# An attention and feed-forward block on one core: heads in 64-row tiles, preparation batch by batch through memory, four slots of rows

## What is computed

```
mod = silu(c) @ wmod                      # per batch: sa, ca, ga, sb, cb, gb; |ga|, |gb| at least 0.25
h   = layernorm(x) * (1 + ca) + sa
q, k, v = split(h @ W_qkv + b_qkv)        # 16 heads of 8 channels each
att = softmax(q @ k.T) / sqrt(128)        # per head, 256 x 256
x   = x + ga * (concat(att @ v) @ W_out + b_out)
h   = layernorm(x) * (1 + cb) + sb
hq  = h rounded to a 6-bit grid in blocks of 32 with a scale of their own; the weight likewise
out = x + gb * (hq @ Wq.T + bias)
```

## Time and profile before

| what | us |
|---|---|
| median of 3 runs | 349.7 |
| lowest and highest run | 349.1, 350.29 |
| profiled execution: span from first to last instruction | 349.2 |
| TensorE busy | 304.0 |
| VectorE busy | 239.4 |
| ScalarE busy | 218.5 |
| GpSimd busy | 173.1 |

### The profile page before, as it was taken

The page is one execution under the profiler, slowest core; times in us unless marked ns, Lnnn a source line. Parts: engine busy times, 40 slices in busy tenths (PEclk is TensorE's granted clock), DMA queues, the critical chain, the costliest instruction groups (busy, mean ns, idle before and its releaser), DMA issues.

```text
span 349.2 us, 8125 instructions
## 1 busy us (share of the span) xinstructions
PE 304.0 (87%) x2506; PEld 216.6 (62%) x2506; DVE 239.4 (69%) x580; ACT 218.5 (63%) x404; POOL 173.1 (50%) x336
## 2 busy tenths in 40 slices
PE   3635698999899997999799997999899989999952
PEld 1204585767576765677576856677676758686521
DVE  4584587578856894779557992779677955886334
ACT  8683055876567765776477654776677645667720
POOL 4360133266736662566636672567556442546540
PEclk9955569999989998999899996999999987999995
DMA  4155365436552555345542555245544554001000
GB/s 132 32 110 115 112 178 111 113 110 174 107 132 93 159 107 122 104 154 101 112 100 94 168 116 120 90 151 103 113 126 139 107 109 126 32 19 34 18 17 15
DMA packets 23700, 36.46 MB, mean 104 GB/s; under 512 B 3422, under 2 KB 10734, under 8 KB 23670
## 3 DMA queue, kind: packets, MB, share of 16 engines
q1 hardware_dynamic: 23302, 35.43, 40.4%
q0 software_dynamic: 368, 0.66, 1.1%
HBM read 9.25 MB, written 2.13 MB: 33 GB/s over the span
## 4 chain that ended last, share of the span: by engine, by line
PE 40%; SPq 29%; DMA 16%; POOL 4%; issue 4%; DVE 3%; ACT 2%; DVEq 0%; ACTq 0%; POOLq 0%
SPq L326 24%; PE ps_o L903 10%; PE ps_p L888 9%; PE ps_p L874 8%; DMA qk_parts<-qk_parts 7%; DMA q_pad<-maxT 7%; PE ps_pre L930 3%; POOL qk_parts L371 2%; SPq L412 2%; PE ps_post L960 2%; SPq L401 2%; PE ps_o L946 1%; PE ps_post L974 1%; PE ps_post L968 1%; DMA q_pad<-qk_parts 1%
## 5 line engine op out<-in xcount | busy, mean ns | idle before, releaser
L762 DVE TENSOR_REDUCE neg_max<-ps_p 128x2 f32<-128x512 f32 x256 | 167.3, 685 | 72.7 <-PE ps_p L874 72.3
L629 ACT ACTIVATE probs<-ps_p 128x512 f32<-128x512 f32 x256 | 145.6, 595 | 82.1 <-PE ps_p L888 79.9
L874 PE MATMUL ps_p<-k_rep,q_pad 96*128 96x256 f32 x512 | 128.2, 338 | 12.1 <-DMA q_pad<-qk_parts 11.7
L888 PE MATMUL ps_p<-q_pad,k_rep 98*128 98x256 f32 x512 | 108.4, 296 | 12.5 <-DMA q_pad<-maxT 12.5
L874 PEld LDWEIGHTS ps_p<-k_rep,q_pad 96*128 96x128 f32 x512 | 84.6, 205 | 46.4 <-issue 35.0
L888 PEld LDWEIGHTS ps_p<-q_pad,k_rep 98*128 98x128 f32 x512 | 82.5, 198 | 16.8 <-issue 14.1
L903 PE MATMUL ps_o<-probs,v_aug 128*32 128x256 f32 x1024 | 82.3, 407 | 0.2 <-ACT probs L629 0.2
L903 PEld LDWEIGHTS ps_o<-probs,v_aug 128*32 128x32 f32 x1024 | 22.6, 112 | 20.2 <-issue 3.1
L530 POOL TENSOR_TENSOR wout_b<-wout_sc,modb 128x128 f32<-128x128 f32 x16 | 7.3, 459 | 49.7 <-DMA modb<-mod_rows_dram 49.6
L494 POOL CAST max_parts<-neg_max 128x16 fp32r<-128x16 f32 x32 | 6.3, 198 | 39.9 <-DVE neg_max L762 39.2
L356 POOL TENSOR_TENSOR hq<-h,rs 128x256 fp8e4<-128x256 f32 x15 | 9.3, 617 | 25.0 <-DVE rs L808 12.8
(11 more groups left out here) (107 smaller groups left out, 356.1 us busy)
## 6 DMA issues: line engine op xcount, KB each, us to landing
q_pad<-qk_parts SPq DMA_DIRECT2D x123, 64.0 KB
qk_parts<-qk_parts SPq DMA_DIRECT2D x14, 512.0 KB, 3.5
k_rep<-qk_parts SPq DMA_DIRECT2D x31, 192.0 KB
modb<-mod_rows_dram SPq DMA_DIRECT2D x16, 256.0 KB, 3.7
x_early<-in_L_attn_x_dram SPq DMA_DIRECT2D x8, 256.0 KB, 3.4
x_late<-in_L_attn_x_dram SPq DMA_DIRECT2D x8, 256.0 KB, 3.4
out_dram<-out_sb SPq DMA_DIRECT2D x16, 128.0 KB, 1.9
k_rep<-qk_parts SPq DMA_DIRECT2D x15, 128.0 KB
```

What stands on the lines that cost most here:

```text
L629: act.activation(probs[:, v % 2, u % 4, :], ps_p2[:, u % 2, :], ACT.Exp).then_inc(exp_done, 1)
L762: dve.tensor_reduce(neg_max[:, half, :, h % HALF], ps_p1[:, P1_BANK[h], :].rearrange("p (q k) -> p q k", q=QT), AX_X, ALU.max, negate=True ...
L874: ins = pe.matmul(ps_p1[:, P1_BANK[h], t * T:(t + 1) * T], q_pad[0:ROWS, par, h, e, t * P:(t + 1) * P], k_rep[0:ROWS, par, g, e, :], start ...
L888: ins = pe.matmul(ps_p2[:, u % 2, t * T:(t + 1) * T], k_rep[0:ROWS + 2, par, g, e, t * P:(t + 1) * P], q_pad[0:ROWS + 2, par, h, e, :], st ...
```

## The change

- **Row tiles.** Each head has 64 rows of its own: 32 rows of q and k parts (four combinations of parts, 8 channels), rows that stay at zero in q and at one in k, and two rows of maxima, 62 and 63. Even heads lie on partitions 0 to 63, odd heads on 64 to 127. `scores1` uses 62 rows, `scores2` 64. `q_rows` and `k_rows` replace `q_pad` and `k_rep` and have four slots, one per batch.
- **Order.** `scores1` runs 20 heads ahead (`LEAD`) where it ran 16 ahead. Both kinds go through the heads in the order 0, 2, 4, 6, 1, 3, 5, 7 and so on (`HEAD`), the matmuls of both kinds alternate one by one, and all other TensorE work stands behind every second head. `values` now comes in 16 instructions throughout.
- **Preparation.** Statistics, normalisation, q, k and their parts run per batch, in tiles of 256 tokens, three batches ahead of the step. x is loaded once and stays (`x_all`). Batches 0 and 1 are prepared ahead of the loop, batch 0 alone first, with x scaled by VectorE.
- **Layout.** SyncE stores each batch's parts in memory off chip (`parts_dram`) and reads them back from there with two DMAs for q and four for k, which also double them. The maxima of half a batch are placed by two DMAs.
- The modulation rows have four buffers (two before), and the loop is written out in full, without registers.

```diff
-GROUPS = [(0, 3), (3, 3), (6, 2), (8, 3), (11, 3), (14, 2)]
-ROWS = 96
-P1_BANK = [0, 1, 2, 0, 1, 0] + [2, 0, 1] * 3 + [2]
+QUAD = 4 * D
+ROWS1 = 62
+ROWS2 = 64
+LEAD = 20
+RING = 4
+P1_BANKS = 3
+P2_BANKS = 2
+FIRST = 2
+HEAD = [8 * (u // 8) + 2 * (u % 4) + (u % 8) // 4 for u in range(16)]
...
+    parts_dram = nc.dram_tensor("parts_dram", [NB, 2, 2, D, 2, HALF, T], F32, kind="Internal").ap()
...
-        qk_parts = sb("qk_parts", [P, 2, 2, 4, TP], F32R)
-        q_pad = sb("q_pad", [P, 2, H, 2, T], F32R)
-        k_rep = sb("k_rep", [P, 2, len(GROUPS), 2, T], F32R)
+        x_all = sb("x_all", [P, NB, QT, E])
+        qk_parts = sb("qk_parts", [P, 2, 2, 2, T], F32R)
+        q_rows = sb("q_rows", [P, RING, HALF, T], F32R)
+        k_rows = sb("k_rows", [P, RING, HALF, T], F32R)
...
+        def at1(b, s):
+            return divmod(16 * b + s + LEAD, 16)
...
+            def store_part(c, kind):
+                if c < FIRST:
+                    sp.wait_ge(first_low, 2 * c + kind + 1)
+                else:
+                    sp.wait_ge(low_ready, 2 * (c - FIRST) + kind + 1)
+                sp.dma_start(parts_dram[c, kind].rearrange("r d u i t -> i (r d) u t"),
+                             qk_parts[:, c % 2, kind, :, :].bitcast(F32)).then_inc(parts_stored[kind], 16)
+            def lay_out(c, kind):
+                wait(sp, (parts_stored[kind], 16 * (c + 1)), (p2_full, 16 * (c - RING + 1)))
+                if c < RING:
+                    sp.wait_ge(rows_filled[c], 2)
+                for r in range(2):
+                    part = parts_dram[c, kind, r].rearrange("d u i t -> d u (i t)")
+                    if kind == 0:
+                        dst = q_rows[64 * r:64 * r + QUAD, c % RING, :, :].rearrange("a i t -> a (i t)")
+                        sp.dma_start(dst.bitcast(F32), part.unsqueeze(2).to_broadcast([D, 2, 2, HALF * T])
+                                     ).then_inc(laid_out[c % RING], 16)
+                    else:
+                        for u in range(2):
+                            dst = k_rows[64 * r + u:64 * r + QUAD:2, c % RING, :, :].rearrange("a i t -> a (i t)")
+                            sp.dma_start(dst.bitcast(F32), part[:, u:u + 1, :].to_broadcast([D, 2, HALF * T])
+                                         ).then_inc(laid_out[c % RING], 16)
...
+            for b in range(-1, NB + 2):
+                c = b + 3
...
+                if has(b + 1) and b >= 0:
+                    load_modb(b + 1)
+                if has(b + 1):
+                    place_max(b + 1, 0)
+                if has(b - 2):
+                    store(b - 2)
+                if in_steps(c):
+                    store_part(c, 0)
+                    store_part(c, 1)
+                    lay_out(c, 0)
+                    lay_out(c, 1)
+                if has(b + 1):
+                    place_max(b + 1, 1)
...
+            def scores1(b, s, t):
+                h = HEAD[s]
+                r, i, slot = h % 2, h // 2, b % RING
+                ins = pe.matmul(ps_p1[:, (16 * b + s) % P1_BANKS, t * T:(t + 1) * T],
+                                q_rows[64 * r:64 * r + ROWS1, slot, i, t * P:(t + 1) * P],
+                                k_rows[64 * r:64 * r + ROWS1, slot, i, :], start=True, stop=True)
...
+                for s in range(0, 16, 2):
+                    for u in (s, s + 1):
+                        if has1(b, u):
+                            before_scores1(*at1(b, u))
+                            scores1(*at1(b, u), 0)
+                        if has(b):
+                            before_scores2(b, u)
+                            scores2(b, u, 0)
+                        if has1(b, u):
+                            scores1(*at1(b, u), 1)
+                        if has(b):
+                            scores2(b, u, 1)
```

More of the change, by code:

```diff
@@ L263, in adaln_block @@
         out_stored = sem("out_stored")
[L266 to L278, removed]
-        def after(batches, per=1, extra=0, total=NB):
-            value = per * batches + extra if extra else per * batches
-            return min(value, per * total) if isinstance(batches, int) else value
@@ L375, in adaln_block, with scale_x @@
+        def scale_x(eng, c):
+            for n in range(QT):
+                ins = eng.tensor_scalar(xhat[:, c % 2, n, :], x_all[:, c, n, :], nm1[:, c % 2, n:n + 1],
+                                        rstd1[:, c % 2, n:n + 1], ALU.add, ALU.mult)
+            ins.then_inc(xhat_ready, 1)
         block = ctx.enter_context(nc.Block())
@@ L599, in save_qk @@
-            def save_qk(p, par, kind, full, saved, bank=ps_pre):
-                wait(act, (full, after(p + 1, total=NPAIR)), (low_ready, after(p, 2, total=NPAIR)),
-                     *[landed(g, p - 1) for g in range(len(GROUPS))])
-                bias = bqkv_col[:, kind:kind + 1]
-                act.activation(qk_full_sb[:, kind, :], bank[:, :], ACT.Identity, bias=bias).then_inc(saved, 1)
-                if isinstance(p, int) and p == 0:
-                    act.activation(qk_parts[:, 0, kind, HIGH[kind], :],
-                                   bank[:, :].unsqueeze(1).to_broadcast([P, 2, TP]),
-                                   ACT.Identity, bias=bias).then_inc(saved, 1)
-                else:
-                    act.activation(qk_parts[:, par, kind, 0, :], bank[:, :], ACT.Identity, bias=bias
-                                   ).then_inc(saved, 1)
@@ L789, in stats2 @@
             def stats2(b):
-                wait_apart(dve, (st2_done, after(b + 1)))
+                wait(dve, (st2_done, b + 1))
                 for n in range(QT):
@@ L907, in values, with transpose_x @@
                     ins.then_inc(pv_done, 1)
-            def transpose_x(p, b):
-                wait(pe, (xhat_ready, after(p + 1, total=NPAIR)), (maxT_saved, after(b + 1, 2, 1)))
-                if isinstance(p, int) and p == 1:
-                    pe.wait_ge(q_saved, 2)
-                for n in range(4):
-                    ins = pe.transpose(ps_pre[:, n * P:(n + 1) * P], xhat[:, n, :], ident[:, :])
+            def transpose_x(c, *before):
+                wait(pe, (xhat_ready, c + 1), *before)
+                for n in range(QT):
+                    ins = pe.transpose(ps_pre[:, n * P:(n + 1) * P], xhat[:, c % 2, n, :], ident[:, :])
@@ L925, in project_v, with project_qk @@
                                     wqkv_sb[:, 2 * E:3 * E], start=True, stop=True)
                 ins.then_inc(v_full, 1)
-            def project_qk(p, par, kind, full, bank, *before):
-                wait(pe, (hT_saved, after(p + 1, 2, total=NPAIR)), *before)
-                pe.matmul(bank[:, :], wqkv_sb[:, kind * E:(kind + 1) * E], hT[:, par, :], start=True, stop=True
+            def project_qk(c, kind, full, dst, *before):
+                wait(pe, (hT_saved, c + 1), *before)
+                pe.matmul(dst, wqkv_sb[:, kind * E:(kind + 1) * E], hT[:, c % 3, :], start=True, stop=True
@@ L1040, in _ @@
-            run_pipeline(pe, pair_step)
+            pe.wait_ge(wqkv_loaded, 16 * 4)
+            for c in range(FIRST):
+                transpose_x(c, (hT_saved, c))
+                project_qk(c, 0, q_full, ps_p2[:, 0, 0:T], (first_low, 2 * c - 1))
+                project_qk(c, 1, k_full, ps_p2[:, 1, 0:T], (first_low, 2 * c))
+                if c == 0:
+                    pe.matmul(ps_o[0:NB, :], cT[:, :], wmod_sb[:, 2 * E:6 * E], start=True, stop=True
+                              ).then_inc(rows_full, 1)
```

838 lines of the change are left out of this document (378 added, 460 removed).

## The result

The changed kernel takes 311.67 us (median of 4 runs, 311.31 to 312.73), where the kernel before took 349.4 beside it (349.06 to 350.29): a ratio of 0.892, with an interval of 0.887 to 0.896. The forecast was 292.6, its range 274 to 320; the forecast's own case ended at 308.

The account below looks back on a forecast made before the run. TensorE, 87% busy, was taken as the bound, then three engines tied together. Start 39.5, first two steps 28.5, eleven steps 167.2, two more 28.4, last 11.3, end 17.2: 292.1, plus 0.5 offset, 292.6 us; range 274 to 320.

Parts of the forecast that it names:

- the forecast's own case: Whole kernel: a step of 14.2 to 16.2 us, so 278 to 308 us in all; chance 0.63.
- rival (a): Scores on TensorE: row tiles don't overlap, 326 us, or 309 to 315 for half an overlap; chance 0.17.
- Row tiles: Scores on TensorE: two matmuls in different row halves run side by side, 3.84 us less per batch if fully overlapped.
- TensorE's work of 13.6: TensorE per batch after the change: 11.5 us plus preparation and 0.8 for changes of shape, 13.6 in sum.
- VectorE 13.6, ScalarE 12.9: Work per batch after the change: VectorE 12.64 us plus first-norm statistics; ScalarE 10.53 plus hT and four saves.
- GpSimd, "no bound": GpSimd per batch: 10.9 us of work, taken not to bound the step.
- T = 15.2: Length of a step in us, taken between 13.6 and 16.2, with some 0.3 for TensorE's waits for saves.
- Layout, "cost nothing": Trip of rows and maxima through memory: a chain of 12.0 us against 14.2 available, slack 2.2.
- Rival (c): Layout: the trip through memory sets the step at 19.8 us, 362 us in all; chance 0.05.
- Start: Before the steps: first scores at 23 us, second-kind scores at 39.5, bounds 36 and 43.
- End: After the last scores: 17.2 us stay as in the kernel before.
- Rival (b): Steps: the engines even out better, a step of at most 14.1 us, 276 us or less; chance 0.13.

Follow-up runs that it names:

- same_half: Changed kernel with heads exchanged within a pair, so both score kinds use the same 64-row half, and the exponential scaled by 2^-6: 367.91 us.
- Norm_early: Changed kernel with the next batch's normalisation on GpSimd moved from the step's end to ahead of its wait for VectorE's statistics: 305.21 us.
- pool_late: Changed kernel with one spare 0.73 us add on GpSimd per step, 15 times, ahead of the next batch's normalisation: 325.27 us.
- x_late: Changed kernel with the load of 12 batches of x issued behind batch 1's layout, not ahead of batch 1's store: 310.27 us.
- best: Changed kernel with next-batch normalisation and second-half maxima split earlier in GpSimd's queue, and x's load behind batch 1's layout: 303.43 us.
- plus_dve: Changed kernel with one spare 128 x 256 add on VectorE behind the work of place 13, 15 times: 312.76 us.
- lead28: Changed kernel with first-kind scores running 28 heads ahead instead of 20, the two kinds again in different halves: 367.99 us.

## Why the prediction was right, and where it was off

The profiled run took 311.46. From 292.6 it is 18.9 away: start 2.6, steps 13.1, end 1.9, offset 1.3. It lies in the range of 274 to 320, but above the 278 to 308 of the forecast's own case, and in the band of rival (a), which did not happen. The mechanism was foreseen, the number is held by the width of the range.

- **Row tiles: right.** 3.84 per batch, complete, shown by the start times and by same_half. The Trainium skill's page "TensorEngine Tiling (Array Packing)", section Key Properties, says that different tiles can load weights and multiply in parallel, and the trace agrees, with starts within 0.01 of each other. The estimate from the Trainium skill's page "TensorE: Matmul & The Clock Gate", Part 3, which left 1.2 of it on TensorE, does not hold here: pairs of two tiles follow each other at 0.12, the pace of single matmuls. What the forecast leaned on was weaker than it read. The values do not "overlap almost fully": four of them start within 0.02, but four follow four at 0.21, and sixteen hold the engine 1.00, where a full overlap would take 4 x 0.12 + 0.19 = 0.67. That the scores did better was luck.
- **TensorE's work of 13.6: 0.4 too low.** Same_half gives 14.0. q and k came as forecast (two starts 0.53 apart, 1.1). The changes of shape were counted too few: full-array work between two blocks of scores now pays its own way in and out. The projection of V holds the engine 0.64 from start to start, where it took 0.37 before, and the transposed output 0.37 for 0.14.
- **VectorE 13.6, ScalarE 12.9: right,** 13.7 and 12.8. VectorE is 86% busy in a step, as the forecast's sign asked, but below TensorE and not level with it. A save of 256 columns took 0.478, I had 0.47.
- **GpSimd, "no bound": the term that failed.** Its amount was right (10.9 forecast, 11.0 measured), the conclusion wrong. It was read as an amount only, and left out of the layout of a step by places. The place behind heads 2 and 3, for which the forecast laid out 1.4 on TensorE and 1.9 at most, took 2.88 (153.49 to 156.37): 0.90 of it is waiting for GpSimd that the profile names, 1.2 by the same place in same_half (2.18, less 0.48 for the overlap). Norm_early takes 0.50 of that away and shortens the step by 0.54; pool_late adds 0.73 and lengthens it by 0.70.
- **T = 15.2, measured 16.0.** Forecast as 13.6 and 1.6 of ties, measured as 14.0 and 2.0. That the ties came out near is partly luck: the list by places adds up to 14.5 for VectorE where its own sum was 13.6, and it has no GpSimd. The eleven steps make 8.8 of the 13.1; the first two and the last three, which the forecast gave only as sums (28.5, 28.4, 11.3), the rest.
- **Layout, "cost nothing": right.** TensorE waits 0.2 us in all for placed maxima. A trip through memory from store issue to load issue took 4.5 for q (161.78 to 166.24) and 4.8 for k (163.70 to 168.51) where I had 3.9. Rival (c) is out.
- **Start.** First scores 24.39 for 23; second kind 42.1 for 39.5. The load of x ahead of batch 1's store was in the forecast, but not the half clock until 50 us, which makes TensorE's work there long enough to matter. X_late gives 1.4 back.
- **End.** 19.1 for 17.2. I took the length from before; the last transposes of normalised values stand behind another batch's feed-forward (296.19, with a wait of 0.61), and TensorE is again at half clock.
- **Offset.** I set 0.5, the distance of the median (349.7) from the profiled span (349.2), but these are two different executions. Every run here shows 1.8 between its own span and time (311.46 and 309.7).

Rival (a), at 309 to 315 for half an overlap, names the measured time for a wrong reason: the overlap is whole, and half of its gain waits elsewhere. Had only the time been read, that rival would have looked confirmed. Rival (b) is out, since no full step came under 15.3 in any version.

## What to carry to other kernels

When the bound engine gets faster, lay out a step of every engine by places, the half-idle ones too. What counts is not their busy share but what stands behind a wait in their queue and has a reader on the bound engine; work that hangs on nothing belongs in front of the wait. And where two causes would give the same time, look for the row that tells them apart (here, the start times of two neighbouring matmuls) before the time is believed.

## What the runs showed of the hardware

- Two matmuls of 64-row tiles in different halves start within 0.01 us of each other, and two such pairs 0.12 apart (0.21 at half clock), as far as single matmuls in one half. Only the first pair of a block takes longer, 0.22.
- Without the overlap the half clock lasted much longer: windows of same_half stand at 0.50 until 106 us and at 1.00 from 124, where the changed kernel was at full clock from about 50. From 50 us on TensorE was busy without a pause in all of it (18.00 of 18.00 from 88 to 106). Its second L455 stands at 120.35 where the changed kernel's stands at 85.42, 35 us of the 56 that its span is longer, and two steps without overlap explain 8 of them at most. Why the half clock lasted so long is open.
- The granted clock in the rows and the matmuls can disagree. X_late's page shows 9 in all slices of the start, and its first 16 scores took the same 4.76 us as in the changed kernel, where the row says 5; the second to the sixth start 0.21 apart in both:

```profile
23.72 4.76 PE L822 MATMUL ps_p<-k_rows,q_rows 62*128 62x256 f32 x16 [7.63 <-DMA k_rows<-parts_dram]
```

The trace of x_late holds no clock record ahead of 48.8 us, and the row prints full clock where it has none. In the traces of best, plus_dve, pool_late and lead28 they begin at 48 us or later too, so that mean clocks of 0.98 and 0.92 of like kernels don't mean different clocks. The spacing of known matmuls is the surer clock.
